# A third state buffer in a selective scan, and one of four token tiles of its inputs from matmuls with a diagonal of B

## The reference

```python
dt = softplus(dt @ dt_proj_w.T + dt_proj_b)
A = -exp(A_log)
def step(h, inps):
    dt_t, x_t, B_t, C_t = inps
    dA = exp(dt_t[..., None] * A)
    h = h * dA + (dt_t * x_t)[..., None] * B_t[:, None, :]
    y = einsum('bdn,bn->bd', h, C_t)
    return (h, y)
_, ys = lax.scan(step, h0, xs)
y = y + xc * D_param
y = y * silu(z)
mamba_out = y @ out_proj_w.T
```

## Time and profile before

| | us |
|---|---|
| median of 3 runs | 651.34 (651.04 to 652.55) |
| the profiled execution | 652.32 |
| its span, first to last instruction | 650.6 |
| busy: PE, DVE, ACT, POOL | 586.3, 464.3, 398.2, 295.1 |

### The profile page before, as it was taken

The page is one execution under the profiler, slowest core; times in us unless marked ns, Lnnn a source line. Parts: engine busy times, 40 slices in busy tenths (PEclk is TensorE's granted clock), DMA queues, the critical chain, the costliest instruction groups (busy, mean ns, idle before and its releaser), DMA issues.

```text
span 650.6 us, 10823 instructions
## 1 busy us (share of the span) xinstructions
PE 586.3 (90%) x3597; PEld 453.7 (70%) x3597; DVE 464.3 (71%) x770; ACT 398.2 (61%) x876; POOL 295.1 (45%) x232
## 2 busy tenths in 40 slices
PE   4999679778898789999999999999999999998773
PEld 2654568677787678798898889899864555655441
DVE  6989989999899965734425543543574688999985
ACT  4689899999899974733214231321556565768543
POOL 6032689999799994122222134233113232134201
PEclk9999799999899999999999999999999999999898
DMA  8001642111121106254414441411430000000001
GB/s 279 2 1 37 199 183 56 50 57 57 36 64 49 49 2 273 76 218 162 170 33 161 163 170 33 159 44 33 131 145 1 2 1 0 1 2 1 1 0 65
DMA packets 18191, 51.42 MB, mean 79 GB/s; under 512 B 3778, under 2 KB 9539, under 8 KB 16484
## 3 DMA queue, kind: packets, MB, share of 16 engines
q1 hardware_dynamic: 15172, 41.43, 18.2%
q0 software_dynamic: 2688, 7.34, 3.8%
q10 hardware_dynamic: 288, 2.10, 0.8%
HBM read 45.95 MB, written 4.92 MB: 78 GB/s over the span
## 4 chain that ended last, share of the span: by engine, by line
PE 62%; ACT 20%; DVE 8%; issue 5%; DMA 2%; POOL 1%; POOLq 0%; DVEq 0%; ACTq 0%
PE ps L2055 14%; ACT arena L651 11%; PE ps L2063 8%; ACT arena L662 8%; PE ps L2128 8%; PE ps L2117 4%; PE ps L2149 3%; PE ps L1954 2%; PE ps L1903 2%; PE ps L1713 2%; PE ps L2078 2%; PE ps L1704 2%; PE ps L2164 2%; DVE arena L1256 1%; PE ps L1725 1%
## 5 line engine op out<-in xcount | busy, mean ns | idle before, releaser
L440 POOL TENSOR_TENSOR arena<-arena 128x1024 f32<-128x1024 f32 x64 | 151.0, 2373 | 12.2 <-DVE arena L1256 8.6
L1256 DVE TENSOR_TENSOR_SCAN arena<-arena,ps 128x1024 f32<-128x1024 f32 x64 | 146.2, 2286 | 13.3 <-POOL arena L440 8.4
L2055 PEld LDWEIGHTS ps<-arena 128*128 128x128 f32 x924 | 106.1, 192 | 5.3 <-issue 4.2
L2055 PE MATMUL ps<-arena 128*128 128x128 f32 x924 | 107.4, 276 | 1.0 <-DVE arena L1354 0.3
L1859 PE MATMUL ps<-ident,arena 128*128 128x128 f32 x512 | 70.8, 283 | 27.8 <-ACT arena L662 19.0
L833 ACT ACTIVATE arena<-ps 128x256 f32<-128x256 f32 x63 | 24.1, 383 | 106.7 <-PE ps L2055 101.4
L651 ACT ACTIVATE arena<-arena,a_neg 128x510 f32<-128x510 f32 x128 | 84.6, 710 | 4.0 <-DVE arena L1256 3.9
L1859 PEld LDWEIGHTS ps<-ident,arena 128*128 128x128 f32 x512 | 57.5, 145 | 39.3 <-ACT arena L662 34.0
L662 ACT ACTIVATE arena<-arena,b_tok 128x512 f32<-128x512 f32 x128 | 84.5, 710 | 0.0
L1872 PE MATMUL ps<-ident,arena 128*128 128x128 f32 x512 | 67.8, 275 | 0.5 <-DVE arena L1265 0.5
L1872 PEld LDWEIGHTS ps<-ident,arena 128*128 128x128 f32 x512 | 58.7, 142 | 1.3 <-DVE arena L1265 1.2
(11 more groups left out here) (293 smaller groups left out, 1001.7 us busy)
## 6 DMA issues: line engine op xcount, KB each, us to landing
arena<-in_w_moe SPq DMA_DIRECT2D x8, 2176.0 KB, 9.2
arena<-c_dram SPq DMA_DIRECT2D x32, 256.0 KB, 3.1
arena<-in_w_o ACTq DMA_DIRECT2D x1, 2048.0 KB, 12.2
arena<-in_w_qT SPq DMA_DIRECT2D x1, 2048.0 KB, 9.2
arena<-moe_out SPq DMA_DIRECT2D x8, 256.0 KB, 4.6
arena<-in_w_q SPq DMA_DIRECT2D x1, 2048.0 KB, 10.0
x<-in_x SPq DMA_DIRECT2D x2, 512.0 KB, 4.6
arena<-in_w_in SPq DMA_DIRECT2D x2, 512.0 KB, 5.9
```

The costliest lines, as they stand in the source:

```text
L440: pool.tensor_tensor(in_chunks(hC[:, unit % 2, :]), in_chunks(h[:, unit % 2, :]), c_bc[:, m % C_BUFS, :].unsqueeze(1).to_broadcast([P, 2, ...
L1256: nc.vector.tensor_tensor_scan(h[:, k, :], dA[:, k, :], ps[:, 2 * k:2 * k + 2, :].rearrange("p a b -> p (a b)"), 0.0, ALU.mult, ALU.add).t ...
L2055: ins = nc.tensor.matmul(ps[:, bank, c * P:(c + 1) * P], w13[:, k, chunk * P:(chunk + 1) * P], xT[:, k, :], start=(k == 0), stop=(k == KD ...
```

## The change

1. h has three buffers, `unit % 3`, at 8, 12 and 34 KB. Before it had two, at 8 and 12. DVE's scan of a unit waits for the product of three units before (`hc_done`), not two.
2. Of the four token tiles of a unit's inputs only three (`ROW_TILES`) are still multiplied by B on ACT and transposed on PE. For the fourth ACT makes the diagonal matrix of B's 128 values (`b_diag`, identity times B, 128x128, two buffers in the space that the smaller `sdtx` leaves), and PE computes dtxT.T @ b_diag, which is the transposed and scaled tile in one matmul. `dtxT` is read directly by PE then, so PE waits for it (`dtxT_done`).

```diff
+ROW_TILES = HALF_TILES - 1
...
-        sdtx, h = [view(0, [HALF_TILES, DI]), view(155, [HALF_TILES, DI])], view(8, [2, T])
+        sdtx, h = [view(0, [ROW_TILES, DI]), view(155, [ROW_TILES, DI])], [view(8, [T]), view(12, [T]), view(34, [T])]
+        b_diag = [view(6, [P]), view(7, [P])]
...
-                pool.tensor_tensor(in_chunks(hC[:, unit % 2, :]), in_chunks(h[:, unit % 2, :]),
+                pool.tensor_tensor(in_chunks(hC[:, unit % 2, :]), in_chunks(h[unit % 3]),
...
                 for i in tiles:
+                    if i == ROW_TILES:
+                        nc.scalar.activation(b_diag[m % 2], ident[:, :], ACT.Identity,
+                                             scale=b_tok[:, HALF_TILES * half + i, n:n + 1]).then_inc(s["sdtx_ready"], 1)
+                        continue
...
-                if unit >= 2:
-                    dve.wait_ge(s["hc_done"], unit - 1)
-                nc.vector.tensor_tensor_scan(h[:, k, :], dA[:, k, :], ps[...], 0.0,
+                if unit >= 3:
+                    dve.wait_ge(s["hc_done"], unit - 2)
+                nc.vector.tensor_tensor_scan(h[unit % 3], dA[:, k, :], ps[...], 0.0,
...
                 pe.wait_ge(s["sdtx_ready"], HALF_TILES * (m + 1))
+                pe.wait_ge(s["dtxT_done"], HALF_TILES * half + HALF_TILES)
...
-                        ins = nc.tensor.transpose(ps[...], sdtx[m % 2][:, i, c * P:(c + 1) * P], ident[:, :])
+                        if i < ROW_TILES:
+                            ins = nc.tensor.transpose(dst, sdtx[m % 2][:, i, c * P:(c + 1) * P], ident[:, :])
+                        else:
+                            ins = nc.tensor.matmul(dst, dtxT[:, HALF_TILES * half + i, c * P:(c + 1) * P], b_diag[m % 2], start=True, stop=True)
```

More of the change, by code:

```diff
@@ L1253, in scan_of @@
                 dve.wait_ge(s["da_ready"], unit + 1)
-                if unit >= 2:
-                    dve.wait_ge(s["hc_done"], unit - 1)
-                nc.vector.tensor_tensor_scan(h[:, k, :], dA[:, k, :], ps[:, 2 * k:2 * k + 2, :].rearrange("p a b -> p (a b)"), 0.0,
+                if unit >= 3:
+                    dve.wait_ge(s["hc_done"], unit - 2)
+                nc.vector.tensor_tensor_scan(h[unit % 3], dA[:, k, :], ps[:, 2 * k:2 * k + 2, :].rearrange("p a b -> p (a b)"), 0.0,
                                              ALU.mult, ALU.add).then_inc(s["scan_done"], 1)
@@ L1852, in inputs_of @@
                 m, pair = divmod(unit, 2)
+                half = m // NS
                 pe.wait_ge(s["sdtx_ready"], HALF_TILES * (m + 1))
+                pe.wait_ge(s["dtxT_done"], HALF_TILES * half + HALF_TILES)
                 if unit >= 2:
@@ L1858, in inputs_of @@
                     for i in range(HALF_TILES):
-                        ins = nc.tensor.transpose(ps[:, 2 * (unit % 2) + k, i * P:(i + 1) * P], sdtx[m % 2][:, i, c * P:(c + 1) * P], ident[:, :])
+                        dst = ps[:, 2 * (unit % 2) + k, i * P:(i + 1) * P]
+                        if i < ROW_TILES:
+                            ins = nc.tensor.transpose(dst, sdtx[m % 2][:, i, c * P:(c + 1) * P], ident[:, :])
+                        else:
+                            ins = nc.tensor.matmul(dst, dtxT[:, HALF_TILES * half + i, c * P:(c + 1) * P], b_diag[m % 2], start=True, stop=True)
                 ins.then_inc(s["dbx_ready"], 1)
```

## The result

| | before | after |
|---|---|---|
| median us (first 4 runs each) | 651.19 (650.61 to 652.55) | 644.79 (641.80 to 645.67) |
| profiled execution, span | 652.32, 650.6 | 644.48, 642.7 |

The ratio is 0.9891 with an interval of 0.9855 to 0.9926. Two later series of five runs of the same kernel give 0.9875 (0.9857 to 0.9893) and 0.9878 (0.9858 to 0.9898). So the change is faster by some 7 us by the first ratio and some 8 us by the two later ones, with medians of 643.6 and 644.2 against 651.6 and 652.0 on the same chips. The forecast was a gain of 5.3 us and a time of 646.0, with a lower end of 644.6.

A forecast was written before the change was run, and what follows sets the result against it. ACT and the h buffer loop were taken to bound the scan together, POOL next. Gains 2.6 (units 3 to 33) + 1.0 (border) + 1.9 (39 to 61) + 0.2 (61 to 63) - 0.4 (beginning) = 5.3: 646.0 us, range 644.6 to 649.4.

The forecast's parts named there:

- Two coincident limits: In the scan, ACT's 4.90 us and the h buffer loop's 4.88 for two units; either edit alone meets the other limit.
- ACT's price: The short 128x128 activation costs ACT 0.28 us from start to start, between bounds of 0.18 and 0.61.
- PE's price: A diagonal matmul costs PE two records, 0.22 us, where a transpose costs 0.11; slower rival: four transposes, chance 0.06.
- POOL's pace: In the scan outside the skips, POOL's products start 2.34 us apart, against 2.45 before.
- The rival with POOL at its full duration: In the scan POOL bounds at 2.375 us a unit; gain 3.6 us or less, time 648; chance 0.21.
- Skips: Units 4 to 11 and 36 to 43 carry skip matmuls; PE bounds there at 2.42 us a unit.
- the second half: Units 39 to 61, 22 steps: 53.71 us become 51.8, gain 1.9.
- The border: Products 33 to 39, 18.12 us before: product 34 waits 1.3 us instead of 2.25, gain 1.0.
- The slow patch: PE's eight transposes at 166.62 take 1.80 us instead of 1.09 or less; assumed to stay.
- The beginning: Up to unit 3's product: four more PE records cost 0.6 us; the product comes 0.4 later.
- The tail: Behind the scan, PE work waiting for the last product: the whole gain carries to the end, no further gain.
- the second case: The rival with POOL bounding at its duration, 2.375 us a unit: time 648, chance 0.21; used for the range's upper end.

The follow-up runs named there:

- experiment 1: The kernel before with the third h buffer alone, inputs unchanged: 650.65 us, ratio 0.9983.
- experiment 2: The change without its third h buffer (diagonal matmuls alone, two h buffers): 651.92 us, ratio 1.0005.
- experiment 4: The change with ACT's short activation made long again, writing the diagonal four times over (128x512): 650.67 us, ratio 0.9978.
- experiment 5: The change with two of the four token tiles made by diagonal matmuls: 646.86 us, ratio 0.9933.
- experiment 11: The change with the skips of each half eight units later: 643.99 us, ratio 0.9875.
- experiment 8: The kernel before with the first half of the first output projection moved behind the last sum in PE's queue: 651.48 us, ratio 0.9994.
- experiment 9: The kernel before with the first half of the first output projection between the last two sums in PE's queue: 650.95 us, ratio 0.9981.
- experiment 3: The change itself, timed again beside its two halves against the kernel before: 643.63 us, ratio 0.9875.

## Why the prediction was wrong in its size, and what in it was right

**Two coincident limits: right.** ACT's 4.90 and the loop's 4.88 us were read from before's rows, and experiments 1, 2 and 4 each put back one of the two: 73.47, 73.42 and 73.47 us for units 3 to 33, against 70.55 without either. Only both edits together reach POOL.

**ACT's price: right by luck.** It is 0.29 us from start to start, for 0.28. But the 0.28 was the whole duration of another row, L865's, taken as the time from start to start. The short activation lasts 387 ns, not 278, and is overlapped by its successor by about 0.1 us, as the long ones are; the two errors cancel. Also, 0.612 - 0.28 is 0.33 us, not the 0.4 that ACT was to get back at the beginning.

**PE's price: right.** A diagonal matmul leaves two records at 0.11 us. The rule of the Trainium skill (TensorE: Matmul & The Clock Gate, Terms), transpose mode four times faster for FP32, is not what this kernel shows: two records against one, with the same spacing. By it experiment 5 would have stood at 3.5 us a unit; it stood at 2.65.

**POOL's pace: right to 0.01 us,** 2.33 instead of 2.34, which is 0.5 us over 52 steps. The rival with POOL at its full duration fell. My argument against it, that product 63 with no scan beside it takes 2.34 us and the others 2.37, was one row: in the fourteen traces product 63, always without a scan beside it, lasts 2.34 to 2.44.

**Skips: half right, and that half by luck.** I had PE as the limit in 12 counted units. In the first half the total fits, but 0.4 of its 0.6 us fall on product 6 alone and the rest on three steps; in the second half it was nothing. A limit 0.08 us above the pace must first use up PE's lead: in the first half only the last three of the eight units show the excess, at either place of the skips (in the change and in experiment 11), product 6 apart. That it lasts for all eight in the second half fits with a greater lead behind the border; no run tests that by itself.

**The border: the wait was right, the total depends on the clock.** Product 34 waits 1.30 us for scan 34 (forecast 1.3), and the step to it takes 3.66 us instead of 4.62. The next step takes 4.06 instead of 3.74, the four behind it 9.31 instead of 9.76, and together that makes 1.1. The slow patch stayed, as I had assumed. PE idled 1.52 us before the inputs of unit 36, and the 3.4 us behind were granted 0.50, the 1.2 GHz level; eight sums took 1.73 us where 1.04 is usual:

```profile
157.39 2.48 DVE L1271 TENSOR_TENSOR arena<-ps,arena 128x512 f32<-128x512 f32 x4 [1.09 <-PE ps L1884]
...
162.22 0.80 PE L1869 MATMUL ps<-ident,arena 128*128 128x128 f32 x3 [1.52 <-DVE arena L1262]
...
164.31 1.73 PE L1884 MATMUL ps<-ident,arena 128*128 128x128 f32 x8
```

```profile
162.30:165.70 3.40, 3.40 (x17) 3.40 (x18) 3.10 (x2) 3.40 (x6) 2.22 (x1) 0.50 0.17 53
165.70:200.00 34.30, 34.02 (x305) 33.33 (x303) 33.01 (x16) 33.68 (x59) 33.79 (x15) 1.00 0.18 55
```

But the patch isn't always there. In experiments 8 and 9, whose scans and border are those of before, the clock stayed at 1.00 behind the same idle time of PE. The window from 158 to 173 us and the inputs at 166.6 (1.80 us in before), in experiment 8:

```profile
158.00:173.00 15.00, 10.87 (x87) 9.16 (x85) 14.27 (x10) 13.13 (x22) 12.38 (x6) 1.00 0.13 45
...
166.60 1.07 PE L1859 MATMUL ps<-ident,arena 128*128 128x128 f32 x8 [1.51 <-DVE arena L1256]
```

There the step to product 35 takes 2.33 us instead of 3.74, and the whole border 16.70. So 1.4 of before's 18.12 us are the clock's. The same window was granted 0.89 in before, in the three traces of the change (borders of 16.97 to 17.03) and in experiment 11 (16.72). Experiment 5, with two tiles from diagonals and a granted clock of 1.00 there, took 15.99. Against a before whose clock stays up the change as traced gains nothing at the border. A gain of 1.1 forecast as 1.0 is therefore partly luck, and how often the clock falls in either kernel these few profiles can't say.

**The beginning: wrong by 0.9 us, and not settled.** I expected product 3 later by 0.4; it came 0.5 earlier. The four traces with before's beginning have it at 88.45, 88.94, 88.30 and 87.25 us, eight with the change's between 87.36 and 88.70, so the spread is as large as the term. PE was slow in both profiles, but in the change only from 73.6 to 77.0 us, in before from 71.2 to 78.0.

**The tail: this step failed.** "Behind the scan the chain goes through PE work that waits for the last product; nothing there is held by a transfer begun before, so I carry all of it to the end." I looked for what could take the gain back behind the scan and took the tail as fixed. It held a wait of PE for ACT, 1.2 us long. The third h buffer lets DVE run ahead of POOL and ACT's last decays with it, and so ACT's late gates are done in time. The buffer does most of it: experiment 1 has 18.74 us and experiment 4, with the buffer and a long activation, 18.53; experiment 2, with the short activation alone, has 19.51. With both it is 18.25, and experiment 9 has nearly all of it by an edit of its own (18.49). The term of the sum that was mis-sized is this one, 0 for 1.2 us. The beginning adds 0.9, the second half 0.5, the first 0.3 and the border 0.1, less the 0.6 us lost far behind the scan in the first profile: that is 7.8 for 5.3, but for rounding. These 0.6 us were not in experiment 3 (from the last projection to the end 392.6 us, before 392.4), and the traces with 21 tiles spread from 390.7 to 393.0 there: I take them for noise.

**The range.** Its upper end was summed up wrongly: the second case with nothing from the border and 0.8 us lost at the beginning gives 651.34 - 2.2 = 649.1, not 649.4. Its lower end left no room for a gain behind the scan, and that is where the time went below it.

## What to carry to other kernels

When an engine is full and a buffer loop beside it has the same period, each edit alone measures as nothing; look for the second limit before an edit is thrown away, and test the pair. A buffer more, or an engine that is freed, lets work run ahead, and that pays where something is waited for once, at borders and tails (0.7 us in the tail with the buffer alone, 1.2 with both): follow the queues to the last instruction, not only to the end of the steady stretch. A short excess on an engine costs nothing as long as its lead lasts (five of eight units here), and its whole length after that. And before a gain at one place is put down to an edit, look whether the same code takes the same time there in other traces: here one border took 18.12 and 16.70 us.

## What the runs showed of the hardware

- At a granted clock of 1.00 an f32 matmul of 128x128 by 128 columns leaves two records of PE, 0.11 us apart, a transpose of the same size one; turns between them in a queue cost nothing that shows (a unit of 24 records with its turns takes 2.65 us).
- ACT's activation of 128x128 f32 from SBUF lasts 387 ns and delays its successor by 0.29 us; one of 512 elements lasts 707 to 715 and delays it by 0.61.
- POOL's product and DVE's scan ran at their old speed with both nearly always busy: 2375 and 2275 ns, before 2375 and 2287. The last product, with no scan beside it, was no faster as a rule (2344 to 2438 ns in fourteen traces).
- Behind 1.51 or 1.52 us of idle time of PE at the border the granted clock fell to 0.50 in before and stayed at 1.00 in experiments 8 and 9, with the same code there; the fall made the border 1.4 us longer. In experiment 5 it stayed at 1.00 as well.
- Runs of one kernel spread more than most of the single edits are worth: before took from 648.50 to 653.59 us in 29 runs on one chip. The three of them with a mean granted clock of 0.991 took 648.50, 649.17 and 650.04 us, the one at 0.983 took 653.39.
